# Reading two neighbouring PSUM banks with one instruction: score maxima of two heads (self and cross attention) and cross exponentials of two heads

## The reference

```python
# layer 0: self attention with mask, cross attention to 77 keys, MLP
s = einsum('bqhd,bkhd->bhqk', q, k) * scale          # 1024 x 1024, masked
a = softmax(where(mask, s, min)); self_out = a @ v
cross = softmax(qc @ kc.T * scale) @ vc              # 1024 x 77
# layer 2: the same without mask, 1024 keys, then an MLP
# layer 3: cross attention from x to the context, 77 keys
```

## Time and profile before

| what | value |
|---|---|
| median of 3 runs | 3469.8 us (3466.66 to 3474.9) |
| profiled execution, its own time | 3466.48 us |
| its span, first to last instruction | 3464.7 us |
| mean granted TensorE clock | 0.953 of full speed |
| TensorE busy | 3150.7 us |
| VectorE busy, instructions | 1823.9 us, 3812 |
| ScalarE busy, instructions | 1464.3 us, 2645 |

### The profile page before, as it was taken

One profiled execution on the slowest core, in us unless ns is written; L12 is line 12 of the kernel. 1 busy time (PEld: TensorE's weight loads), 2 busy tenths in 40 slices (PEclk: granted clock), 3 DMA queues, 4 the chain that ended last, 5 costly groups with the idle time before them and its releaser, 6 DMA issues.

```text
span 3464.7 us, 51568 instructions
## 1 busy us (share of the span) xinstructions
PE 3150.7 (91%) x20564; PEld 1858.1 (54%) x20564; DVE 1823.9 (53%) x3812; ACT 1464.3 (42%) x2645; POOL 257.2 (7%) x278
## 2 busy tenths in 40 slices
PE   6899999999889999998488989999999999999887
PEld 3555666656576656665234445454454545554464
DVE  4876554562412332323377765757757577557343
ACT  0343444444312222221046645555456555565433
POOL 1100010010100000000100001001100101001010
PEclk9998999999889999999689989999999999999899
DMA  5200000003000000000420020001200000000000
GB/s 168 91 1 6 8 21 1 15 14 96 16 23 0 1 0 1 1 0 5 143 67 32 26 75 24 15 20 44 86 13 22 28 28 25 13 28 31 1 1 13
DMA packets 78707, 104.29 MB, mean 30 GB/s; under 512 B 18688, under 2 KB 52208, under 8 KB 78204
## 3 DMA queue, kind: packets, MB, share of 16 engines
q1 hardware_dynamic: 78468, 100.93, 9.0%
HBM read 72.05 MB, written 28.86 MB: 29 GB/s over the span
## 4 chain that ended last, share of the span: by engine, by line
PE 80%; DVE 9%; ACT 4%; DMA 2%; issue 2%; SPq 1%; POOL 1%; DVEq 0%; ACTq 0%; POOLq 0%
PE ps L976 73%; PE ps L1189 3%; DVE max_halves L1680 2%; ACT big L2024 2%; DMA k_parts<-qk_parts 1%; PE ps L1316 1%; PE ps L1180 1%; DVE row_max_cross L1846 1%; DMA q_parts<-qk_parts 1%; PE ps L1168 1%; DVE xn_tok L1752 1%; DVE bn_stats L1716 1%; ACT probs L2083 1%; SPq L877 1%; DVE bn_stats L1739 1%
## 5 line engine op out<-in xcount | busy, mean ns | idle before, releaser
L2024 ACT ACTIVATE big<-ps 128x512 f32<-128x512 f32 x1280 | 692.7, 595 | 668.3 <-PE ps L976 667.8
L1680 DVE TENSOR_REDUCE max_halves<-ps 128x1 f32<-128x512 f32 x1024 | 650.3, 683 | 239.9 <-PE ps L976 232.4
L976 PE MATMUL ps<-k_groups,q_blocks 32*128 32x512 f32 x2048 | 449.4, 464 | 89.8 <-DVE qk_parts L1815 33.8
L976 PE MATMUL ps<-q_blocks,k_groups 32*128 32x512 f32 x2048 | 423.4, 468 | 4.0 <-DVE qk_parts L1815 2.0
L976 PE MATMUL ps<-big,probs 128*32 128x512 f32 (+1 forms) x2688 | 383.6, 613 | 12.3 <-ACT big L2024 5.8
L976 PE MATMUL ps<-weights_mlp,big 128*128 128x256 f32 (+1 forms) x1248 | 333.5, 419 | 2.5 <-ACT big L2095 2.5
L976 PEld LDWEIGHTS ps<-q_blocks,k_groups 32*128 32x128 f32 x2048 | 175.9, 187 | 297.2 <-issue 282.9
L976 PEld LDWEIGHTS ps<-weights_mlp,big 128*128 128x128 f32 x1248 | 234.0, 190 | 83.6 <-issue 57.9
L976 PEld LDWEIGHTS ps<-k_groups,q_blocks 32*128 32x128 f32 x2048 | 188.8, 190 | 158.4 <-ACT big L2024 55.6
L1722 DVE TENSOR_TENSOR x_tok<-ps,x_tok 128x512 f32<-128x512 f32 x112 | 77.2, 690 | 312.1 <-PE ps L976 311.9
L2083 ACT ACTIVATE probs<-ps 77x512 f32<-77x512 f32 x384 | 196.2, 591 | 96.0 <-PE ps L976 95.7
(11 more groups left out here) (233 smaller groups left out, 3970.7 us busy)
## 6 DMA issues: line engine op xcount, KB each, us to landing
q_blocks<-q_parts SPq DMA_DIRECT2D x64, 256.0 KB
q_parts<-qk_parts SPq DMA_DIRECT2D x48, 256.0 KB
k_parts<-qk_parts SPq DMA_DIRECT2D x32, 256.0 KB
k_groups<-k_parts SPq DMA_DIRECT2D x16, 512.0 KB
weights_mlp<-in_L_xcond_mlp_W SPq DMA_DIRECT2D x5, 1024.0 KB, 5.3
weights_mlp<-in_L_xcond_W_mlp SPq DMA_DIRECT2D x5, 1024.0 KB, 5.1
x_tok<-in_x SPq DMA_DIRECT2D x4, 1024.0 KB, 9.6
out_y<-x_tok SPq DMA_DIRECT2D x8, 512.0 KB, 3.2
```

The source lines that it names most:

```text
L976: return pe.matmul(out, lhsT, rhs, start=first, stop=last)
L1680: dve.tensor_reduce(NMP[:, e, j, qt, hf:hf + 1], PS[:, bank, :], AX.X, ALU.max, negate=True).then_inc(R.frees(key), 1)
L2024: act.activation(PB[:, score % 2, j, :], PS[:, R.bank(key), :], ACT.Exp, scale=SCALE).then_inc(R.frees(key), 1)
```

## The change

It lets one instruction read two neighbouring banks where the keys are maxima (`max`, `cm`) or cross exponentials (`cs`). In the numbering, an even head and the odd head behind it form a pair if the even one's bank isn't the ring's last (6), since the pair's banks must lie side by side; otherwise both stay single. The bank numbers of the keys are the same as before. What changes is the counting: only the last key of a pair (its closer) raises `ring_full` and `ring_free`, once, on the closer's bank, and every wait for a key becomes a wait for its pair's closer. So PE's `take` of key n waits for the pair that key n-7 is in.

```diff
+        PAIRED = ('max', 'cs', 'cm')
...
-                n = 0
+                n, ends, self.tells, self.closers = 0, [0] * 7, {}, set()
                 for tok in self.order:
-                    for key in self.entries(tok):
-                        self.number[key] = n
-                        n += 1
+                    keys = self.entries(tok)
+                    while keys:
+                        size = 2 if keys[0][0] in PAIRED and keys[0][-1] % 2 == 0 and n % 7 < 6 else 1
+                        self.closers.add(keys[size - 1])
+                        n += size
+                        ends[(n - 1) % 7] += 1
+                        for i, key in enumerate(keys[:size]):
+                            self.number[key] = n - size + i
+                            self.tells[n - size + i] = ((n - 1) % 7, ends[(n - 1) % 7])
+                        keys = keys[size:]
...
             def full(self, key):
-                return self.ring_full[self.number[key] % 7], self.number[key] // 7 + 1
+                i, count = self.tells[self.number[key]]
+                return self.ring_full[i], count
...
+            def freed_before(self, n):
+                i, count = self.tells[n - 7]
+                return self.ring_free[i], count
...
                     if n >= 7:
-                        pe.wait_ge(R.ring_free[n % 7], n // 7)
+                        pe.wait_ge(*R.freed_before(n))
...
                 def done(last, key):
-                    last.then_inc(R.fills_up(key), 1)
+                    if key in R.closers:
+                        last.then_inc(R.fills_up(key), 1)
...
-                        dve.tensor_reduce(NMP[:, e, j, qt, hf:hf + 1], PS[:, bank, :], AX.X, ALU.max, negate=True).then_inc(R.frees(key), 1)
+                        dve.tensor_reduce(NMP[:, e, j:j + size, qt, hf], ps, AX.X, ALU.max, negate=True).then_inc(R.frees(key), 1)
...
                     elif kind == "cm":
-                        for j in range(HG):
+                        for first, key, size in R.together([tok + (j,) for j in range(HG)]):
...
                             dve.wait_ge(*R.full(key))
+                            src, dst = PS[:, R.banks(first, size), 0:4 * NC], NMC[:, hf, g // 2, 32 * j:32 * (j + size)]
...
                     elif kind == "cs":
-                        for j in range(HG):
-                            key = tok + (j,)
+                        for first, key, size in R.together([tok + (j,) for j in range(HG)]):
+                            j = first[-1]
                             act.wait_ge(*R.full(key))
-                            act.activation(PC[0:NC, j, :], PS[0:NC, R.bank(key), :], ACT.Exp, scale=SCALE).then_inc(R.frees(key), 1)
+                            act.activation(PC[0:NC, j:j + size, :], PS[0:NC, R.banks(first, size), :], ACT.Exp, scale=SCALE).then_inc(R.frees(key), 1)
```

More of the change, by code:

```diff
@@ L406, in closing, with together, banks @@
                 return sorted(self.number, key=self.number.get)[-7:]
+            def together(self, keys):
+                out, here = [], []
+                for key in keys:
+                    here.append(key)
+                    if key in self.closers:
+                        out.append((here[0], here[-1], key[-1] - here[0][-1] + 1))
+                        here = []
+                return out
+            def banks(self, first, n):
+                return slice(self.bank(first), self.bank(first) + n)
             def bank(self, key):
@@ L411, in full @@
             def full(self, key):
-                return self.ring_full[self.number[key] % 7], self.number[key] // 7 + 1
+                i, count = self.tells[self.number[key]]
+                return self.ring_full[i], count
             def freed(self, key):
-                return self.ring_free[self.number[key] % 7], self.number[key] // 7 + 1
+                i, count = self.tells[self.number[key]]
+                return self.ring_free[i], count
+            def freed_before(self, n):
+                i, count = self.tells[n - 7]
+                return self.ring_free[i], count
             def fills_up(self, key):
-                return self.ring_full[self.number[key] % 7]
+                return self.ring_full[self.tells[self.number[key]][0]]
             def frees(self, key):
-                return self.ring_free[self.number[key] % 7]
+                return self.ring_free[self.tells[self.number[key]][0]]
             def qk_steps(self, b, m):
@@ L1668, in normalize, with fill @@
                     dve.tensor_tensor(dst, src[:, :, :, 0:HD], rec.rearrange("p t (j a) -> p t j a", a=1).broadcast_to([P, 4, HG, HD]), ALU.mult).then_inc(last, 1)
-                def fill(key):
-                    _, n, s, j = key
+                def fill(first, key, size):
+                    _, n, s, j = first
                     b, g, qh = R.block(n)
-                    bank, e = R.bank(key), g % 2
+                    e, ps = g % 2, PS[:, R.banks(first, size), :]
                     dve.wait_ge(*R.full(key))
                     if R.few:
-                        c = 32 * j + 16 * (1 - e) + 4 * qh + 2 * s
-                        dve.tensor_reduce(NM[:, 2 * qh + e, c:c + 2], PS[:, bank, :].rearrange("p (t n) -> p t n", t=2), AX.X, ALU.max, negate=True).then_inc(R.frees(key), 1)
+                        c = 16 * (1 - e) + 4 * qh + 2 * s
+                        dst = NM[:, 2 * qh + e, 32 * j:32 * (j + size)].rearrange("p (j c) -> p j c", j=size)[:, :, c:c + 2]
+                        dve.tensor_reduce(dst, ps.rearrange("p j (t n) -> p j t n", t=2), AX.X, ALU.max, negate=True).then_inc(R.frees(key), 1)
                     else:
                         qt, hf = 4 * qh + s // NH, s % NH
-                        dve.tensor_reduce(NMP[:, e, j, qt, hf:hf + 1], PS[:, bank, :], AX.X, ALU.max, negate=True).then_inc(R.frees(key), 1)
-                        if (s, j) == (R.per - 1, 1):
+                        dve.tensor_reduce(NMP[:, e, j:j + size, qt, hf], ps, AX.X, ALU.max, negate=True).then_inc(R.frees(key), 1)
+                        if key[2:] == (R.per - 1, 1):
                             dve.wait_ge(*R.freed(key))
@@ L1694, in slot @@
                     for half in range(2):
-                        for key in R.fills(fills, half):
-                            fill(key)
+                        for first, key, size in R.together(R.fills(fills, half)):
+                            fill(first, key, size)
                     for q in tails:
@@ L1836, in region_dve @@
                         _, x, b, g, hf = tok
-                        for j in range(HG):
-                            key, c = tok + (j,), 32 * j + 16 * (1 - g % 2)
+                        for first, key, size in R.together([tok + (j,) for j in range(HG)]):
+                            j, c = first[-1], 16 * (1 - g % 2)
                             dve.wait_ge(*R.full(key))
+                            src, dst = PS[:, R.banks(first, size), 0:4 * NC], NMC[:, hf, g // 2, 32 * j:32 * (j + size)]
                             if R.l == 2:
-                                src = PS[:, R.bank(key), 0:4 * NC].rearrange("p (t a n) -> p t a n", t=2, a=2)
-                                dst = NMC[:, hf, g // 2, 32 * j:32 * j + 32].rearrange("p (a c) -> p c a", a=2)[:, 2 * (g % 2):2 * (g % 2) + 2, :]
-                            else:
-                                src = PS[:, R.bank(key), 0:4 * NC].rearrange("p (t n) -> p t n", t=4)
-                                dst = NMC[:, hf, g // 2, c:c + 4]
+                                src = src.rearrange("p j (t a n) -> p j t a n", t=2, a=2)
+                                dst = dst.rearrange("p (j a c) -> p j c a", j=size, a=2)[:, :, 2 * (g % 2):2 * (g % 2) + 2, :]
+                            else:
+                                src = src.rearrange("p j (t n) -> p j t n", t=4)
+                                dst = dst.rearrange("p (j c) -> p j c", j=size)[:, :, c:c + 4]
                             dve.tensor_reduce(dst, src, AX.X, ALU.max, negate=True).then_inc(R.frees(key), 1)
```

## The result

The changed kernel takes 3507.5 us (median of four runs, 3505.6 to 3512.0), the kernel before, with one more run beside them, 3472.4. The ratio is 1.0103 with a 95% interval of 1.0089 to 1.0117: about 35 us slower. Forecast was 3480 us, 10.5 us slower, in a range of 3459 to 3510. The side, the place and the prices came out as written. The size did not: it is more than three times the sum. The time lies outside the forecast's own 3473 to 3490; it is inside the stated range only because that reaches up to a rival, the dearer read, which turned out false. That is luck.

What follows compares the result with a forecast made beforehand. TensorE, 91% busy and 80% of the chain, was taken as the bound, moved by its waits for PSUM banks. Losses of +21.0 and gains of -10.5 us net +10.5 on the 3469.8 us median: 3480, range 3459 to 3510.

Steps and rivals of the forecast that it cites:

- the sum: All priced waits and gains over the kernel: +21.0 and -10.5, net +10.5 us.
- the dearer read: Rival, all merged reads: two banks cost two lone instructions, about +40 us, 3510 us; chance 0.08.
- The rule of firsts and seconds: PE's bank waits: a pair's second bank comes free slightly earlier (58 or 70 ns), its first 323 to 537 ns later.
- The prices and counts: Merged reads: 1220 and 792 ns for maxima, 1017 for exponentials; 554 maxima, 166 cross maxima, 160 cross exponential pairs.
- The waits of 0.94 and 0.87 us: PE's waits: cross maxima about 0.94 us instead of 0.62; the slot behind cross exponentials near 0.87.
- PE's busy time unchanged: TensorE: listed among the signs that the forecast is right; no change in its busy time.
- +10.6 +1.6 -1.3: Cross maxima: 33 firsts at 0.32 us, next slot's last bank 8 times at 0.2, seconds and group ends gaining.
- +5.2 -2.4: Cross exponentials: 12 slots wait 0.43 us longer for the first; 14 waits end 0.12 earlier, 12 end 0.06 earlier.
- +1.6 +2.0 -4.8: Self-attention maxima: three firsts at 0.54 us, firsts with little time to spare, 58 seconds and 10 firsts gaining 0.07 each.
- VectorE's queue: Work behind a pair on VectorE starts about 70 ns earlier; only the chain's part counts, taken as -2 us.
- the throughput wins: Rival, VectorE's and ScalarE's queues: later firsts cost nothing, gains stand alone, -10.5 us, 3459 us; chance 0.15.
- it cancels: Rival, PE's waits: half the losses fall into waits that follow anyway, 10.5-10.5, 3470 us; chance 0.19.

Runs made afterwards that it cites:

- the filled kernels: PE runs unread matmuls before waiting for a cross-maxima group's fourth bank, 35 places: changed kernel (two of 231 columns) 3480.0 us, kernel before (two of 154) 3460.1 us.
- the filled kernel before: Kernel before, all keys single, plus two unread matmuls of 308 columns ahead of the cross-maxima wait at 35 places: 3462.5 us, 0.9971.

## Why the prediction came out as it did

**Right.** The rule of firsts and seconds decides, and against the change. The prices and counts hold to 3 ns and to the piece. The waits of 0.94 and 0.87 us came as 0.97 and 0.88. Weight-load waits for the maxima fell from 91 to 77, as forecast, but not shorter: 50.8 us in 77 is 0.66 us each, where 53.1 in 91 was 0.58. Cross maxima are the place, by the run with them alone.

**Wrong: "PE's busy time unchanged".** The sum priced each wait by its length and nothing else. It had no term for the slower running behind the waits: 28.6 us with the cross maxima alone, 16.6 in the full change, some 15 by the filled kernels. The Trainium skill, page Perfetto Trace Analysis, section Matmul Optimizations, says that the matmul engine scales its power with utilization, so that matmuls should run back to back in batches. The trace agrees: the granted clock went from 1.00 to 0.50 behind the two longer waits above, and the filled kernel before, with more work, is 0.29% faster.

**Too small: the stalls themselves.** They too came out at twice the sum, +22.3 us of idle time. By PE's table of waits, the cross maxima were at +10.6 +1.6 -1.3 = +10.9 us and brought +15.4 (a total of 45.2 against "near 40"): at the first matmuls of a slot that follows such maxima, PE now stands twelve times, mostly 0.2 to 0.6 us, where it stood once. Cross exponentials were at +5.2 -2.4 = +2.8 and brought +5.0. Self maxima were at +1.6 +2.0 -4.8 = -1.2, a gain, and brought +4.5 (18 waits where there were 13); which of the three terms was off wasn't tried. Other waits of PE shrank by 2.6 in sum, where VectorE's queue stood at -2.

**Not settled.** Alone, the exponentials measured +0.12% and the self maxima +0.07%, both with intervals that include no change. The cross maxima alone lose the same time as the full change with half the idle time (+11.4) and more slower running (+28.6); why the two kernels split it so differently isn't shown.

**The rivals.** That the throughput wins falls: VectorE lost 41 us of work and the kernel is slower. The section on Scalar and DVE operations that the prediction set beside it (the Trainium skill, Perfetto Trace Analysis, Optimizing Scalar/DVE Operations) is borne out: at 53% VectorE was not saturated, and the smaller instructions with their earlier releases are worth more. That it cancels falls with the interval. The dearer read named 3510 us, closer to the 3507 than my own figure, but for a wrong cause: the merged instructions take the low price, and cross maxima read singly but let go in pairs lose the same.

## What to carry to other kernels

Before one instruction takes over two buffers' reads, ask of each wait for those buffers whether it is for the first or the second; if for the first and nothing else is ready, the merge costs the time of the second's columns (0.62 us of waiting became 0.97 here). Price a TensorE stall by its length only where the granted clock stays up behind it; look at the clock of the whole stretch, since the slower matmuls behind may cost more than the wait, as they did for the cross maxima alone. What helped most was order, without any pair: other work between producers that use up the ring. It was worth 1.35% here, with PE's idle time behind the cross maxima down from 29.8 to 11.8 us and the time at 1.2 GHz from 326 to 261; the whole order moved, so not all of it need come from those places.

## What the runs showed of the hardware

With waits of mostly 0.97 us where they were mostly 0.62, the granted clock fell behind more of them (43 of 52 instead of 27 of 42); at one such place the same eight matmuls took 1.07 us at 1.00 and 1.73 behind the fall. Matmuls whose results nobody reads, fitted into such waits, raised the mean clock from 0.953 to 0.959 in the profiled executions and made the kernel before faster by 0.29% [0.18, 0.41] and, with shorter ones, 0.27% [0.12, 0.41]. And a VectorE or ScalarE read across two neighbouring PSUM banks ran at the single bank's rate: 1223 ns for 1024 columns (683 for 512), and on ScalarE 1017 ns (591 for 512).
